# Selective scan: products and first-half scans as single instructions of 1024 columns

## The reference, cut to what matters

```python
def _selective_scan(u, delta, A, B_ssm, C_ssm, D):     # b=4, L=1024, dim=256, n=16 states
    h0 = jnp.zeros((b, dim, n), u.dtype)
    def step(h, inp):
        u_t, dt_t, B_t, C_t = inp
        dA = jnp.exp(dt_t[..., None] * A)
        h = dA * h + (dt_t * u_t)[..., None] * B_t[:, None, :]
        y = jnp.einsum('bdn,bn->bd', h, C_t)
        return (h, y)
    ...
    return ys.transpose(1, 0, 2) + u * D
```

## Time and profile before

| | us |
|---|---|
| median of 3 runs | 1764.95 (1760.73 to 1766.72) |
| profiled execution, its own time | 1766.69 |
| its span in the profile | 1764.9 |
| the scan stage, from 117.2 to 545.5 | 428.3 |
| VectorE busy in it | 427.46 |
| GpSimd busy in it | 400.84 |
| ScalarE busy in it | 261.39 |

### The profile page before, as it was taken

The page is one execution under the profiler, slowest core; times in us unless marked ns, Lnnn a source line. Parts: engine busy times, 40 slices in busy tenths (PEclk is TensorE's granted clock), DMA queues, the critical chain, the costliest instruction groups (busy, mean ns, idle before and its releaser), DMA issues. The chain is left out here.

```text
span 1764.9 us, 26058 instructions
## 1 busy us (share of the span) xinstructions
PE 1313.6 (74%) x7183; PEld 715.1 (41%) x7239; DVE 1269.3 (72%) x2564; ACT 874.9 (50%) x1615; POOL 953.9 (54%) x1017
## 2 busy tenths in 40 slices
PE   5847877777779678989351799998898998703638
PEld 2313333333333267889331244443343343303624
DVE  7999999999997452152772988889889886361315
ACT  5846665666665524565241066655565566502310
POOL 1579999999993027343652021213563564774740
PEclk9969999999999869999775799999999999956859
DMA  1038000000000035778323010100110113032325
GB/s 53 0 126 302 1 0 1 1 0 1 0 1 0 6 101 171 206 212 220 101 81 127 32 54 32 56 30 30 61 70 33 43 39 99 10 55 63 97 78 191
DMA packets 124247, 122.77 MB, mean 70 GB/s; under 512 B 29522, under 2 KB 102463, under 8 KB 121720
## 3 DMA queue, kind: packets, MB, share of 16 engines
q1 hardware_dynamic: 102292, 97.47, 18.3%
q0 software_dynamic: 10240, 15.79, 3.0%
q10 hardware_dynamic: 11588, 8.01, 1.4%
HBM read 76.68 MB, written 50.52 MB: 72 GB/s over the span
## 5 line engine op out<-in xcount | busy, mean ns | idle before, releaser
L1885 ACT ACTIVATE t_PT<-t_ps_s 128x1024 f32<-128x1024 f32 (+3 forms) x384 | 294.7, 811 | 236.2 <-PE t_ps_s L2198 235.3
L1910 DVE TENSOR_REDUCE t_negm<-t_ps 128x1 f32<-128x512 f32 (+4 forms) x624 | 368.6, 640 | 49.1 <-PE t_ps L2179 25.8
L464 POOL TENSOR_TENSOR s_HC<-s_H,X 128x512 f32<-128x512 f32 x256 | 321.7, 1288 | 24.9 <-DVE s_H L588 18.6
L2179 PE MATMUL t_ps<-heads 128*128 128x512 bf16 (+3 forms) x720 | 217.1, 338 | 65.3 <-DVE t_identb L1903 36.9
L626 PE MATMUL ps_y<-s_HC,ident 128*128 128x512 f32 x512 | 250.7, 613 | 0.3
L1817 POOL TENSOR_SCALAR_AFFINE_SELECT t_PT<-t_PT 128x512 f32<-128x512 f32 x128 | 84.0, 658 | 301.9 <-ACT t_PT L1885 301.6
L2198 PE MATMUL t_ps_s<-heads 128*128 128x512 bf16 (+3 forms) x760 | 179.8, 329 | 4.9 <-ACT t_PT L1885 2.1
L2179 PEld LDWEIGHTS t_ps<-heads 128*128 128x128 bf16 x768 | 73.6, 99 | 228.2 <-DVE t_negm L1910 146.9
L2213 PE MATMUL t_ps_c<-t_PT,t_VG 128*32 128x512 f32 (+3 forms) x1536 | 164.5, 501 | 1.1 <-ACT t_CT L1847 0.6
L528 ACT ACTIVATE s_dA<-m_DT,s_A 128x512 f32 (+1 forms) x192 | 127.5, 712 | 60.4 <-DVE s_H L588 60.2
L1801 POOL DMA_INDIRECT slots<-X,t_idx_s x128 | 127.6, 997 | 34.6 <-issue 34.6
(11 more groups left out here) (328 smaller groups left out, 2586.1 us busy)
## 6 DMA issues: line engine op xcount, KB each, us to landing
f_w<-in_W_dram SPq DMA_DIRECT2D x93, 256.0 KB, 4.9
y_Y<-token_expert_rows SPq DMA_DIRECT2D x8, 1024.0 KB, 12.4
token_expert_rows<-X SPq DMA_DIRECT2D x42, 192.0 KB, 2.6
heads<-qk_parts SPq DMA_DIRECT2D x42, 192.0 KB
heads<-qk_parts SPq DMA_DIRECT2D x14, 576.0 KB
qk_parts<-p_parts SPq DMA_DIRECT2D x48, 128.0 KB, 2.9
expert_rows<-X SPq DMA_DIRECT2D x27, 192.0 KB, 2.5
f_XS<-expert_rows SPq DMA_DIRECT2D x19, 256.0 KB
```

What stands on the lines that cost most here:

```text
L464: nc.gpsimd.tensor_tensor(HC[:, g % RING, c, :], H[:, g % RING, c, :], C_sb[:, g % RING, :], ALU.mult).then_inc(s_hc, 1)
L1885: nc.scalar.activation(PT[:, n % RP, 2 * p:2 * p + 2, 0:wd], src, ACT.Exp, scale=DK ** -0.5).then_inc(s_exp, 1)
L1910: nc.vector.tensor_reduce(out, ps_1[use % BANKS1][:, 0:h * width].rearrange("p (h k) -> p h k", h=h), AX.X, ALU.max, negate=True).then_inc ...
L2179: mm = nc.tensor.matmul(out[:, u * width:(u + 1) * width], Q[g][:, j + u, qt * P:(qt + 1) * P], K[g][:, j + u, c * CH:c * CH + width], sta ...
```

## The change

Each pair of VectorE and GpSimd products over the two channel halves becomes one instruction over [2, 512] columns (`DU`, the B products, the C products), with the row of B or C repeated by a stride of zero (`row_wide`). `ps_d[k]` and `ps_b[k]` become the two halves of one tile `ps_in[k]` over two PSUM banks. In first halves the two scans also become one over 1024 columns. So that the second half's channels start from zero there, the decay in column 512 must be 0: ScalarE writes it as one column before the exponentials of g = 0, 1 and of the four `BY_POOL` states (`FRESH`), and in all first halves the exponential of channel half 1 leaves that column out. In second halves the scans stay two, each from its own `last`. The waits are joined: a consumer waits for both halves at once, and a semaphore `s_fr` for the written zeros is added to the scans of `FRESH` states. The number of instructions of TensorE and its order stay.

```diff
@@ -394,6 +394,7 @@
     BY_POOL = [g for g in range(N) if g % 4 == 3]
     by_dve = lambda g: g // 4 * 3 + min(g % 4, 3)
     ND = by_dve(N)
+    FRESH = [0, 1] + BY_POOL
     with ExitStack() as ctx:
         sb = lambda n, s, d=F32: ctx.enter_context(nc.sbuf_tensor("s_" + n, s, d))
         sem = lambda n: ctx.enter_context(nc.semaphore(n))
@@ -411,8 +412,8 @@
         diag = sb("diag", [P, 2, P])
         C_sb = keep["X1"][:, 0:RING * CH].rearrange("p (k n) -> p k n", n=CH)
         last = sb("last", [P, 2, NST])
-        ps_b = [bank(f"ps_b{k}") for k in range(2)]
-        ps_d = [bank(f"ps_d{k}") for k in range(2)]
+        ps_in = [ctx.enter_context(nc.psum_tensor(f"ps_in{k}", [P, 2, CH], F32)) for k in range(2)]
+        ps_b = [ps_in[k][:, 1, :] for k in range(2)]
         ps_c, ps_m = bank("ps_c"), bank("ps_m")
         ps_y = [bank(f"ps_y{c}") for c in range(2)]
         s_w = sem("s_weights")
@@ -432,8 +433,9 @@
         s_own = sem("s_own_step")
         s_zt = sem("s_zero_rows")
         zero = keep["X1"][:, T:T + ZERO]
+        s_fr = sem("s_first_decay_zero")
         s_m, s_mc, s_mi = sem("s_b_spread_early"), sem("s_b_copied"), sem("s_input_by_pool")
-        keep["used"] += [s_w, s_sel, s_a, s_b, s_c, s_da, s_cs, s_du, s_in, s_h, s_hl, s_hc, s_y, s_out, s_own, s_m, s_mc, s_mi, s_zt]
+        keep["used"] += [s_w, s_sel, s_a, s_b, s_c, s_da, s_cs, s_du, s_in, s_h, s_hl, s_hc, s_y, s_out, s_own, s_m, s_mc, s_mi, s_zt, s_fr]
 
         ctx.enter_context(nc.allow_non_contiguous_dma(reason="small per-feature vectors"))
         block = ctx.enter_context(nc.Block())
@@ -457,19 +459,17 @@
             def times_c(i, g):
 
                 pool.wait_ge(s_cs, i * N + g + 1)
-                for c in range(2):
-                    pool.wait_ge(s_h, i * 2 * N + 2 * g + c + 1)
-                    if past(i, 1) or g >= RING:
-                        pool.wait_ge(s_y, i * 2 * N + 2 * (g - RING) + c + 1)
-                    nc.gpsimd.tensor_tensor(HC[:, g % RING, c, :], H[:, g % RING, c, :], C_sb[:, g % RING, :], ALU.mult).then_inc(s_hc, 1)
+                pool.wait_ge(s_h, i * 2 * N + 2 * g + 2)
+                if past(i, 1) or g >= RING:
+                    pool.wait_ge(s_y, i * 2 * N + 2 * (g - RING) + 2)
+                nc.gpsimd.tensor_tensor(HC[:, g % RING], H[:, g % RING], row_wide(C_sb[:, g % RING, :], 2), ALU.mult).then_inc(s_hc, 2)
 
             def input_of(i, h, g):
 
                 pool.wait_ge(s_mc, i * len(BY_POOL) + g // 4 + 1)
-                for c in range(2):
-                    if g == BY_POOL[0]:
-                        pool.wait_ge(s_du, i * 2 + c + 1)
-                    nc.gpsimd.tensor_tensor(inp[:, c, :], DU[:, h, c, :], B_sb[:, g // 4 % 2, :], ALU.mult).then_inc(s_mi, 1)
+                if g == BY_POOL[0]:
+                    pool.wait_ge(s_du, i + 1)
+                nc.gpsimd.tensor_tensor(inp, DU[:, h], row_wide(B_sb[:, g // 4 % 2, :], 2), ALU.mult).then_inc(s_mi, 2)
 
             def chunk_of(b, h):
                 for g in range(N):
@@ -488,6 +488,7 @@
             act.wait_ge(s_w, 32)
             nc.scalar.activation(A[:], A[:], ACT.Exp).then_inc(s_a, 1)
             act.wait_ge(s_a, 2)
+            act.wait_ge(s_zt, 1)
 
             def save(g):
 
@@ -521,11 +522,12 @@
                             save(N - 2 + g)
                         else:
                             act.sem_inc(s_own, 1)
+                    out = ps_in[k][:] if g in BY_POOL else dA[:, k]
+                    if h == 0 and g in FRESH:
+                        nc.scalar.activation(out[:, 1, 0:1], zero[:, 0:1], ACT.Copy).then_inc(s_fr, 1)
                     for c in range(2):
-                        out = dA[:, k, c, :]
-                        if g in BY_POOL:
-                            out = (ps_b if c else ps_d)[k][:]
-                        nc.scalar.activation(out, chunk2(DT, c, i), ACT.Exp,
+                        lo = c if h == 0 else 0
+                        nc.scalar.activation(out[:, c, lo:CH], DT[:, c, bass.ds(i * CH + lo, CH - lo)], ACT.Exp,
                                              scale=A[:, c, g:g + 1]).then_inc(s_da, 1)
                     act.wait_ge(s_c, i * N + g + 1)
                     if past(i, 1) or g >= RING:
@@ -554,39 +556,41 @@
 
             def chunk_of(b, h):
                 i = b * 2 + h
-                for c in range(2):
-                    nc.vector.tensor_tensor(DU[:, h, c, :], chunk2(DT, c, i), chunk2(U, c, i), ALU.mult).then_inc(s_du, 1)
+                both = lambda a: a[:, :, bass.ds(i * CH, CH)]
+                nc.vector.tensor_tensor(DU[:, h], both(DT), both(U), ALU.mult).then_inc(s_du, 1)
                 for g in range(N):
                     k = g % 2
                     n = i * 2 * N + 2 * g
-                    made = i * 2 * ND + 2 * by_dve(g)
-                    decay = [dA[:, k, c, :] for c in range(2)]
-                    new = [ps_d[k][:], ps_b[k][:]]
+                    decay, new = dA[:, k], ps_in[k][:]
                     if g in BY_POOL:
-                        decay, new = new, [inp[:, c, :] for c in range(2)]
+                        decay, new = ps_in[k][:], inp
                     else:
                         dve.wait_ge(s_b, i * ND + by_dve(g) + 1)
-                        for c in range(2):
-                            if g == 0:
-                                dve.wait_ge(s_du, i * 2 + c + 1)
-
-                            if past(i, 1) or g >= 2:
-                                dve.wait_ge(s_h, n - 3 + c)
-                            nc.vector.tensor_tensor(new[c], DU[:, h, c, :], ps_b[k][:], ALU.mult).then_inc(s_in, 1)
+                        if g == 0:
+                            dve.wait_ge(s_du, i + 1)
+                        if past(i, 1) or g >= 2:
+                            dve.wait_ge(s_h, n - 2)
+                        nc.vector.tensor_tensor(new, DU[:, h], row_wide(ps_b[k], 2), ALU.mult).then_inc(s_in, 1)
+                    if g in BY_POOL:
+                        dve.wait_ge(s_mi, i * 2 * len(BY_POOL) + 2 * (g // 4) + 2)
+                    else:
+                        dve.wait_ge(s_in, i * ND + by_dve(g) + 1)
+                    dve.wait_ge(s_da, n + 2)
+                    if past(i, 1) or g >= RING:
+                        dve.wait_ge(s_hc, n + 2 - 2 * RING)
+                    if h == 0:
+                        if g >= RING:
+                            dve.wait_ge(s_hl, b * N + g - RING + 1)
+                        if g in FRESH:
+                            dve.wait_ge(s_fr, b * len(FRESH) + FRESH.index(g) + 1)
+                        one = lambda a: a.rearrange("p c n -> p (c n)")
+                        nc.vector.tensor_tensor_scan(one(H[:, g % RING]), one(decay), one(new), 0.0, ALU.mult, ALU.add).then_inc(s_h, 2)
+                        continue
+                    if g < RING:
+                        dve.wait_ge(s_hl, b * N + N - RING + 1 + g)
                     for c in range(2):
-                        if g in BY_POOL:
-                            dve.wait_ge(s_mi, i * 2 * len(BY_POOL) + 2 * (g // 4) + c + 1)
-                        else:
-                            dve.wait_ge(s_in, made + c + 1)
-                        dve.wait_ge(s_da, n + c + 1)
-                        if past(i, 1) or g >= RING:
-                            dve.wait_ge(s_hc, n + c + 1 - 2 * RING)
-                        if h == 0 and g >= RING:
-                            dve.wait_ge(s_hl, b * N + g - RING + 1)
-                        elif h == 1 and g < RING:
-                            dve.wait_ge(s_hl, b * N + N - RING + 1 + g)
-                        nc.vector.tensor_tensor_scan(H[:, g % RING, c, :], decay[c], new[c],
-                                                     last[:, c, g:g + 1] if h else 0.0, ALU.mult, ALU.add).then_inc(s_h, 1)
+                        nc.vector.tensor_tensor_scan(H[:, g % RING, c, :], decay[:, c, :], new[:, c, :],
+                                                     last[:, c, g:g + 1], ALU.mult, ALU.add).then_inc(s_h, 1)
             chunk_of(0, 0)
             chunk_of(0, 1)
             with dve.Fori(1, BATCH) as b:
@@ -603,7 +607,7 @@
                 if past(i, 1) or g >= 2:
                     pe.wait_ge(s_h, i * 2 * N + 2 * (g - 1))
                 if g not in BY_POOL:
-                    nc.tensor.matmul(ps_b[k][:], sel[:, g, :], chunk(G, i), start=True, stop=True).then_inc(s_b, 1)
+                    nc.tensor.matmul(ps_b[k], sel[:, g, :], chunk(G, i), start=True, stop=True).then_inc(s_b, 1)
                 if past(i, 1) or g >= 1:
                     pe.wait_ge(s_cs, i * N + g)
                 nc.tensor.matmul(ps_c[:], sel[:, N + g, :], chunk(G, i), start=True, stop=True).then_inc(s_c, 1)
```

## The result

The changed kernel takes 1779.68 us (median of 5 runs, 1776.07 to 1781.18) where the kernel before takes 1764.95: ratio 1.0091, 95% interval 1.0072 to 1.0110. That is slower, as forecast, by 14.7 us where 22 were named, and inside the range of 1770 to 1797. The profiled execution took 1781.18 us.

What follows compares the result with a forecast made beforehand. VectorE was taken to bound the scan stage. Loop states +17.4, unrolled states +0.8, `DU` +1.5, first scan +0.8 and stage end +1.8 gave +22.3 us, so 1787 against the 1764.95 median; range 1770 to 1797.

Steps and rivals of the forecast that it cites:

- The bound, and starts rather than durations: Scan stage: VectorE is busy in all but 1 us of 428.3, so distances between its instruction starts set the time.
- Merged durations: Lengths of merged instructions: VectorE product 1.20 us, first-half scan about 2.27 us, GpSimd product 2.36 us.
- The wait rides on a register operation: VectorE's loop: the product's wait sits on register operation L581, so merged scans start 0.20 to 0.32 us late; +17.4 us.
- 0.04 everywhere: Rival: the product's wait rides on the scan itself in the loop too, costing 0.04 us; +6.3 us, 1771; chance 0.13.
- the hidden tail: Rival: a scan may start as close behind its product as an independent one; -6.4 us, 1758.6; chance 0.12.
- First halves: First-half scans in the loop: 0.28 us behind the product from state 4 on, 0.32 or 0.20 before; +2.9 us per chunk.
- `DU`: Merged product taken as 2.74 us plus 0.2 until the queue is through; +1.5 us in all, bounds 0 and +3.
- ScalarE's zeros: ScalarE: the first scan waits for both exponentials and a zero column, +0.8 us; the other 23 zeros cost nothing.
- GpSimd's slack: Four second-half states take GpSimd 11.8 us against VectorE's 13.7, so its merged products cost nothing there.
- the two ends: Scan stage's start, first scan waiting for ScalarE, +0.8 us; its end, ScalarE's last copy starting later, +1.8 us.
- that rival: GpSimd becomes the bound if a merged product exceeds 2.7 us; up to 1802; chance 0.09, shared with a longer queue.
- the exposed queue itself: Main case: VectorE's queue work between product and scan is no longer covered; 1780 to 1795 us, chance 0.66.

## Why the prediction was right, point by point

- **The bound, and starts rather than durations.** Right. By mean durations the change should have gained: the two products last 671 and 681 ns (the second in the earlier trace rows), and 96 x (671 + 681 - 1208) ns is 14 us for products alone. By starts it loses, and did.
- **Merged durations.** 1.20, 2.27 and 2.36 us were named; 1208, 2287 and, for GpSimd, 2371 ns measured. Two banks cost nothing.
- **The wait rides on a register operation.** Right in place and kind, and shown from three sides: without register values it is gone (1763.4), with one operation more the scan stage is 6.5 us longer, and in the kernel before the same operation is free. In second halves the size is exact: 0.19 and 0.30 for 0.20 and 0.32. It did not save "0.04 everywhere" or the hidden tail; both rivals fall, since even the smallest gap, 0.04, is no overlap of -0.09.
- **First halves.** The term was sized at 0.28 and measured 0.35, +11.7 us for +8.7; unrolled it was 0.09 for 0.04. The merged scan, which raises its semaphore by 2, has one more event in front of it. With products merged and scans split, where the scan raises by 1, the gap was 0.28 and 0.03. What fits both is that an instruction that raises by 2 carries no wait. The trace of the changed kernel bears this out beyond the scans: none of its 64 merged scans and 160 merged GpSimd products, which raise by 2, carries a wait, while all 96 merged products of VectorE, as wide but raising by 1, carry one, and in the kernel before all 256 scans and all 256 C products do. So it goes with the increment and not with the width; a merged scan that raises by 1 was not run. Of the 3.0 us over the forecast, some 0.75 are the first scan of each first half of the loop, with gaps of 0.75, 0.49 and 0.47 us where 0.32 was named; what they wait for is open.
- **`DU`.** This is the step that failed: "Merged I take 2.74 + 0.2", +1.5 us, was measured as -7.3. The row was there, 2.79 us for two products that take 0.68 each in the first chunk, and I carried its length over as if it were the instructions' own, instead of asking what they wait for. The term is wrong in sign and by 8.8 us; states that cost 4.1 more than named, 22.3 for 18.2, took back half of it, so the stage came out at +18.0 for +22.3. That the sum stayed so near is in part luck, two errors of opposite sign.
- **ScalarE's zeros, GpSimd's slack, the two ends.** Right: +0.8 at the start for +0.8, +2.2 at the end for +1.8, and GpSimd nowhere among VectorE's waits, so that rival falls as well.
- **The number.** 1779.68 lies inside 1770 to 1797, and just below the 1780 to 1795 that were given to the exposed queue itself. The last 3.3 us of the distance to the forecast are stages that the change does not touch, and no credit of the reasoning. The written sum also has small slips: the terms of a loop's second half add up to 3.0 us and not 2.9, those of the unrolled second half to 0.7 and not 0.8. Neither matters for the outcome.

## What to carry to other kernels

Two halves of a tile are worth keeping apart if the second covers, on the same engine, what the consumer of the first has to wait for: completion, events and register operations. Before merging instructions, read the distance of their starts rather than their durations, and count what the queue has to do between the producer's end and the consumer. Merge where no consumer is right behind, or where the instruction has to give way to another engine each time it starts.

## What the runs showed of the hardware that was not expected

- A VectorE instruction with both inputs in SBUF waits until the GpSimd instruction that is running has ended: it takes 0.68 us alone, up to 1.77 beside instructions of 1.27 us, 2.84 beside instructions of 2.37.
- The place of a wait in the program decides whether it costs 0.04 us (on the instruction), 0.09 to 0.14 (an event of its own), or 0.19 to 0.35 (ahead of register operations), measured between the same two instructions.
- Instructions that raise a semaphore by 2 carried no wait in any of 224 cases, on two engines; their waits became entries of the queue in front of them, which cost 0.07 us each where they were exposed.
- One chip took 1916 us for the kernel that others do in 1764. In the four kernels traced there the difference was in the experts' stages and the attention, not in the scan stage.
